# Merged value-output weights of an attention kernel: one block at each layer boundary, or four parts in the layer before

## What is computed

```python
def attn_layer(x, Wqkv, qs, ksc, Wo):
    q, k, v = jnp.split(x @ Wqkv, 3, -1)      # 16 heads of 64
    ...
    out = local_attention(q, k, v)            # softmax(q k) v, windows of 32
    out = out.transpose(0, 2, 1, 3).reshape(b, n, INNER)
    return out @ Wo
for i in range(DEPTH):                        # 6
    x = attn_layer(shift_tokens(x), Wqkv[i], ...) + x
    x = ffn_layer(shift_tokens(x), ...) + x
```

## Time and profile before

| | |
|---|---|
| median of 3 runs | 3483.62 us (3481.26 to 3486.61) |
| the profiled execution | 3489.47 us, its span 3487.7 us |
| mean granted clock of TensorE | 0.986 of full |
| TensorE, VectorE, ScalarE, GpSimd busy | 3341.8, 2797.8, 2306.6, 2258.2 us |
| the recurrence, from the first tanh to the first projection of a layer | 13.8 to 379.8 us |
| the layers | 379.8 to 3487.7 us |

### The profile page before, as it was taken

How to read it: one execution, slowest core, us unless ns; L and a number is a source line. 1 busy time by engine, 2 the same in 40 slices (tenths; PEclk the granted TensorE clock), 3 DMA queues, 4 the chain that set the end, 5 groups by cost and what they waited for, 6 DMA issues and landing times. The chain is left out here.

```text
span 3487.7 us, 101023 instructions
## 1 busy us (share of the span) xinstructions
PE 3341.8 (96%) x42261; PEld 2160.1 (62%) x42261; DVE 2797.8 (80%) x4511; ACT 2306.6 (66%) x4497; POOL 2258.2 (65%) x1364
## 2 busy tenths in 40 slices
PE   8999699999999999999999999999999999999996
PEld 4555366666666666666666666666666666666663
DVE  2333498888898898888898789888898888898983
ACT  2222267777777777777777677776777777777774
POOL 0000267777677777777777677777677776777773
PEclk9999799999999999999999999999999999999999
DMA  2000000100000100001000001000001000000000
GB/s 71 1 1 1 4 11 11 32 11 11 11 13 12 35 11 11 8 17 35 11 11 8 11 17 33 10 11 11 8 17 35 11 11 8 11 17 16 12 11 13
DMA packets 62282, 52.51 MB, mean 15 GB/s; under 512 B 11527, under 2 KB 59397, under 8 KB 61829
## 3 DMA queue, kind: packets, MB, share of 16 engines
q1 hardware_dynamic: 61828, 46.05, 5.1%
HBM read 43.93 MB, written 2.10 MB: 13 GB/s over the span
## 5 line engine op out<-in xcount | busy, mean ns | idle before, releaser
L448 POOL TENSOR_TENSOR cosp<-cosp,rr 128x1024 f32<-128x1024 f32 x384 | 722.6, 1903 | 592.4 <-DVE rr L963 592.3
L458 POOL TENSOR_TENSOR cosp<-cosp,sinp 128x1024 f32<-128x1024 f32 x384 | 902.5, 2370 | 65.9 <-DVE sinp L942 65.9
L543 PE MATMUL ps<-w_qk,xs 128*128 128x512 f32 x1536 | 766.6, 622 | 20.1 <-ACT sq L755 16.5
L644 PEld LDWEIGHTS ps<-px,w_vo 128*128 128x128 f32 x6144 | 701.0, 192 | 57.5 <-ACT px L808 45.7
L644 PE MATMUL ps<-px,w_vo 128*128 128x128 f32 x6144 | 721.4, 276 | 1.9 <-ACT px L808 1.7
L755 ACT ACTIVATE sq<-ps 128x1024 f32<-128x1024 f32 x384 | 392.7, 1023 | 472.9 <-DVE sinp L942 472.9
L939 DVE TENSOR_TENSOR cosp<-ps,tab 128x1024 f32<-128x1024 f32 x384 | 469.3, 1222 | 153.9 <-PE ps L543 152.6
L543 PEld LDWEIGHTS ps<-w_qk,xs 128*128 128x128 f32 x1536 | 264.2, 192 | 387.6 <-issue 378.6
L948 DVE TENSOR_REDUCE ss<-sq 128x16 f32<-128x1024 f32 x384 | 455.3, 1186 | 54.4 <-ACT sq L755 54.3
L942 DVE TENSOR_TENSOR sinp<-ps,tab 128x1024 f32<-128x1024 f32 x384 | 466.4, 1215 | 0.0
L704 PE MATMUL ps<-pT,xtm 32*128 32x512 f32 x3072 | 445.0, 628 | 12.7 <-issue 4.7
(11 more groups left out here) (106 smaller groups left out, 4475.9 us busy)
## 6 DMA issues: line engine op xcount, KB each, us to landing
tab<-in_tab SPq DMA_DIRECT2D x96, 128.0 KB, 2.1
qks<-in_scales SPq DMA_DIRECT2D x96, 128.0 KB, 3.3
w_qk<-in_L_ffn_Wqkv SPq DMA_DIRECT2D x12, 512.0 KB, 6.3
w_v<-in_wv_t SPq DMA_DIRECT2D x6, 512.0 KB, 8.4
w_o<-in_L_ffn_Wo SPq DMA_DIRECT2D x6, 512.0 KB, 9.2
x<-in_L_attn_x SPq DMA_DIRECT2D x16, 128.0 KB, 5.1
out<-w_v SPq DMA_DIRECT2D x16, 128.0 KB, 2.4
w<-in_L_ffn_W SPq DMA_DIRECT2D x6, 341.0 KB
```

The costliest lines, as they stand in the source:

```text
L448: eng.tensor_tensor(v, v, rr[:, B % 2, HEADS * i:HEADS * i + HEADS].unsqueeze(2).to_broadcast([P, HEADS, DH]), ALU.mult).then_inc(rot_read ...
L458: eng.tensor_tensor(cosp[:, A % 2, i, :], cosp[:, A % 2, i, :], sinp[:, i, :], ALU.add).then_inc(rot_added, 1)
L543: t = eng.matmul(ps[:, u, :], xs[:, n % ROUND, :], w_qk[:, n // TILES % 2, i, 512 * u:512 * u + 512], start=True, stop=True)
L644: t = eng.matmul(Y, w_vo[:, i // HP, i % HP, :], px[:, i, :], start=i == 0, stop=i == HEADS - 1)
```

## The change

The block is cut into four parts. For layers 1 to 5 part p of layer L is made in step 32 (L - 1) + 16 + 4 p, so in the first step of each of the last four turns of the layer before. A part has two of the eight 64-row slices, both halves of each: four matmuls into banks G(1) and G(2), 256 columns of each, ahead of that step's Y. One ScalarE copy takes them to `w_vo`, which now has two sets, taken in turn by layers. Layer 0's four parts are made inside the recurrence, at position 24 of chunks 3 to 6, in banks 2 and 6, and VectorE copies them in two instructions each. SyncE asks for the weights of q, k, value and output one turn earlier. To make room, the buffer `xe` of the last turned rows is laid into the output weights' buffer.

```diff
@@ -114,7 +114,7 @@
 LN_STEPS = 3 * TB + 1 + NSTEPS
 POST_STEPS = 1 + LN_STEPS + 3 + LN_STEPS
 KEEP = 512
-AT_OUTPUT, AT_INPUT, AT_XN = 3, 38, 54
+AT_OUTPUT, AT_FUSE, AT_INPUT, AT_XN = 3, 24, 38, 54
 DMA_W1 = 1 + 2 * len(FT)
 DMA_W2 = len(FT) + 1
 
@@ -136,7 +136,7 @@
         w_qk = sb("w_qk", [P, 2, 2, INNER])
         w_v = sb("w_v", [P, HP, D])
         w_o = sb("w_o", [P, HP, D])
-        w_vo = sb("w_vo", [P, 2, HP, D])
+        w_vo = sb("w_vo", [P, 2, 2, HP, D])
         w_1 = sb("w_1", [P, 2 * FF])
         w_2 = sb("w_2", [P, 3, D])
         tab = sb("tab", [P, 2, 4, DH])
@@ -167,7 +167,6 @@
         px = sb("px", [P, HEADS, P])
 
         xc = sb("xc", [P, CH])
-        xe = sb("xe", [P, CH])
         xr = sb("xr", [P, TB, D])
         xn = sb("xn", [P, TB, D])
         xf = sb("xf", [P, CH])
@@ -194,6 +193,7 @@
         t4 = sb("t4", [P, 4, TB])
         b4 = sb("b4", [P, TB], I32)
         fin = w_v.rearrange("p (r j) d -> p r j d", r=2)
+        xe = w_o.rearrange("p k d -> p (k d)")[:, 0:CH]
 
         ps = ctx.enter_context(nc.psum_tensor("ps", [P, 8, 512], F32))
         R = ps[:, 0:2, :]
@@ -293,9 +293,9 @@
             T = (s - lag) // ROUND
             return T if (s - lag) % ROUND == 0 and 0 <= T < TURNS else None
 
-        def layer_of(s):
-            L = (s - 2) // TILES
-            return L if (s - 2) % TILES == 0 and 0 <= L < DEPTH else None
+        def fuse_of(s):
+            L, part = s // TILES + 1, s % TILES // ROUND - 4
+            return (L, part) if s % ROUND == 0 and part >= 0 and L < DEPTH else None
 
         def leaving(s):
             c = (s - 4 * (TURNS - NC) - 15) // ROUND
@@ -402,7 +402,7 @@
                 if L and T % NC == 1:
                     load_1(L)
                     load_2(L)
-                if L + 1 < DEPTH and T % NC == 3:
+                if L + 1 < DEPTH and T % NC == 2:
                     load_qk(L + 1)
                     load_vo(L + 1)
             for c in range(TURNS - FIRST_OUT, NC):
@@ -511,6 +511,18 @@
                 eng.matmul(ps[:, 7, 0:KEEP].rearrange("p (a n) -> p a n", n=P), ident_bf[:, :],
                            ident_bf[:, :].unsqueeze(1).to_broadcast([P, KEEP // P, P]), start=True, stop=True)
 
+            def fuse(L, part):
+                if part == 0:
+                    eng.wait_ge(wv_in, 16 * (L + 1))
+                    eng.wait_ge(wo_in, 16 * (L + 1))
+                if L == 0:
+                    after(eng, vo_evac, part)
+                for i in range(2 * part, 2 * part + 2):
+                    for x in range(2):
+                        rows = slice(64 * x, 64 * x + 64)
+                        t = eng.matmul(ps[:, 5 + x if L else 2 + 4 * x, D * (i % 2):D * (i % 2) + D], w_v[rows, i, :], w_o[rows, i, :], start=True, stop=True)
+                t.then_inc(vo_done, 1)
+
             turn_xn(0)
             eng.wait_ge(abc_out, 1)
             eng.wait_ge(zeroed, 8)
@@ -530,11 +542,14 @@
                     keep_warm()
                     if t == AT_OUTPUT and c:
                         outputs(c - 1)
+                    if t == AT_FUSE and c - 3 in range(4):
+                        fuse(0, c - 3)
                     if t == AT_INPUT and c:
                         turn_input(c - 1)
                     if t == AT_XN and c < NC - 1:
                         turn_xn(c + 1)
             outputs(NC - 1)
+            eng.wait_ge(vo_evac, 4)
 
             def project(n, i):
                 if n % TILES == 0:
@@ -637,27 +652,18 @@
                 if tile(E):
                     eng.wait_ge(px_evac, 3 * (E + 1))
                     eng.wait_ge(px_last, E + 1)
+                    if fuse_of(s):
+                        fuse(*fuse_of(s))
                     if E % TILES == 0:
                         eng.wait_ge(vo_evac, 4 * (E // TILES + 1))
                     after(eng, y_added, E)
                     for i in range(HEADS):
-                        t = eng.matmul(Y, w_vo[:, i // HP, i % HP, :], px[:, i, :], start=i == 0, stop=i == HEADS - 1)
+                        t = eng.matmul(Y, w_vo[:, E // TILES % 2, i // HP, i % HP, :], px[:, i, :], start=i == 0, stop=i == HEADS - 1)
                     t.then_inc(y_done, 1)
-                L = layer_of(s)
-                if L is not None:
-                    eng.wait_ge(wv_in, 16 * (L + 1))
-                    eng.wait_ge(wo_in, 16 * (L + 1))
-                    after(eng, y_added, E + 1)
-                    eng.wait_ge(xt_evac, C + 1)
-                    for i in range(HP):
-                        for x in range(2):
-                            t = eng.matmul(G(2 * x + i // 4)[:, D * (i % 4):D * (i % 4) + D], w_v[64 * x:64 * x + 64, i, :],
-                                           w_o[64 * x:64 * x + 64, i, :], start=True, stop=True)
-                            if i % 4 == 3:
-                                t.then_inc(vo_done, 1)
                 if tile(B):
-                    if L is not None:
-                        eng.wait_ge(vo_evac, 4 * (L + 1))
+                    if fuse_of(s):
+                        L, part = fuse_of(s)
+                        eng.wait_ge(vo_evac, 4 * L + part + 1)
                     eng.wait_ge(rot_ready, 2 * B + 1)
                     turn(B, 0, Q_BANKS)
                 if tile(A):
@@ -828,11 +834,11 @@
                     eng.wait_ge(y_added, ROUND * (T + 1))
                     after(eng, rows_done, T)
                     shifted(xc[:, :].rearrange("p (b t) -> p b t", b=BATCH), xb, slice(0, BATCH), turn_cols(T), turn_cols_before(T), xc_ready)
-                L = layer_of(s)
-                if L is not None:
-                    for k in (0, 2, 1, 3):
-                        eng.wait_ge(vo_done, 4 * L + (2 if k % 2 == 0 else 4))
-                        eng.copy(w_vo[:, k // 2, 4 * (k % 2):4 * (k % 2) + 4, :].rearrange("p i d -> p (i d)"), G(k)).then_inc(vo_evac, 1)
+                if fuse_of(s):
+                    L, part = fuse_of(s)
+                    eng.wait_ge(vo_done, 4 * L + part + 1)
+                    after(eng, y_done, TILES * (L - 1))
+                    eng.copy(w_vo[:, L % 2, :, 2 * part:2 * part + 2, :], ps[:, 5:7, 0:2 * D].rearrange("p x (i d) -> p x i d", d=D)).then_inc(vo_evac, 1)
                 if tile(B):
                     after(eng, sims_done, B)
                     for u, k in enumerate(Q_BANKS):
@@ -869,6 +875,7 @@
 
             def read_result(c):
                 eng.wait_ge(x_updated, DEPTH * NC + c + 1)
+                eng.wait_ge(vo_done, 4 * DEPTH)
                 after(eng, end_turned, c)
                 eng.copy(xe[:, :].rearrange("p (b t) -> p b t", b=BATCH), xa[:, :, 1 + FW * c:1 + FW * c + FW]).then_inc(end_read, 1)
 
@@ -923,6 +930,12 @@
             for c in range(NC - 1):
                 if c:
                     post(c - 1)
+                if c - 3 in range(4):
+                    part = c - 3
+                    eng.wait_ge(vo_done, part + 1)
+                    for x in range(2):
+                        t = eng.tensor_copy(w_vo[:, 0, x, 2 * part:2 * part + 2, :].rearrange("p i d -> p (i d)"), ps[:, 2 + 4 * x, 0:2 * D])
+                    t.then_inc(vo_evac, 1)
                 normalise(c + 1)
             post(NC - 2)
             last = Steps(eng, post_step, (NC - 1) * POST_STEPS)
```

## The result

The change takes 3489.89 us (median of 20 runs, 3483.77 to 3494.02); the kernel before, in as many runs beside it, 3482.07 us (3470.73 to 3488.11). The ratio is 1.002, with a 95% interval of 1.0013 to 1.0028, which is 4.5 to 9.8 us. So the change costs 7.8 us: small, but more than the noise between the two sets of runs.

A forecast was written before the change was run, and what follows sets the result against it. TensorE, busy 96% of the span with almost no gaps, was taken as the bound. 49.0 + 2.5 - 42.3 - 6.5 = +2.7 us against the 3483.62 us median gave 3486.3 us, range 3476 to 3503.

The forecast's parts named there:

- twenty parts: Layers 1 to 5, first step of a turn: each part delays the q transposes 2.45 us, +49.0 us in all.
- recurrence: Layer 0's four parts, chunks 3 to 6: about 0.6 us each in the tanh chain, +2.5 us in all.
- five boundaries: Boundary steps of layers 1 to 5 lose two waits, the burst and following half clock: -42.3 us.
- layer 0's block: Step 2, while the pipeline fills: transposes start earlier without the block, -6.5 us, bounds -7.0 and -5.5.
- The chain: In a part's step, ScalarE copies after square and mask; q transposes wait for it, starting 2.45 us later.
- All of it is in the difference to the clean step: 7.17 to 9.75 us: Boundary steps: everything the change removes was taken as their excess over a 15.53 us step, middle 8.46 us.
- The DMA: Weights asked for one turn earlier: cost nothing, landing in 9.2 us against some 61 us until needed.
- The clock rival: TensorE's twenty stops before the q transposes bring half clock, 1.7 us at nine: +15 us, 3501 us; chance 0.30 (slower).
- the nine stops at L691: Stops of 1.6 to 2.2 us counted in the layers' trace; four said to be followed by slow clock.
- behind Y it is safe: The new stop follows dense Y matmuls, like the first boundary's 2.94 us without slow matmuls; no slow stretch summed.
- Faster through catching up: VectorE and GpSimd use the stops; TensorE recovers 0.6 us or more of each: -9 or more, 3474 us; chance 0.07.
- Faster through an early copy: ScalarE reaches the copy during Y, so a part costs only 0.51 us: -36, 3448 us; chance 0.08.

The follow-up runs named there:

- experiment 1: The change with ScalarE's copy of each part moved ahead of the square of q: 3459.01 us, ratio 0.9932 to the kernel before.
- experiment 2: The change with ScalarE's copy of each part between the square of q and the copy of the transposed x: 3465.99 us, ratio 0.9957 to the kernel before.
- experiment 3: The change with a second ScalarE copy, into a spare tile, ahead of each part's copy in layers 1 to 5: 3511.08 us, ratio 1.0083.
- experiment 4: The change with each part of layers 1 to 5 issuing its four matmuls twice: 3486.62 us, ratio 1.0017 to the kernel before.
- experiment 5: The kernel before, with eleven filler matmuls in each boundary step while TensorE waits for Y's sum: 3470.46 us, ratio 0.9964.
- experiment 7: The kernel of experiment 1, with layer 0's four parts replacing two filler matmuls at their positions in the recurrence: 3453.67 us, ratio 0.9915 to the kernel before.
- experiment 8: The kernel of experiment 7, with layers 1 to 5 made in two parts of eight matmuls instead of four: 3452.52 us, ratio 0.9905 to the kernel before.
- experiment 6: The change with layer 0's weights made in the old block in step 2, no parts in the recurrence: 3492.87 us, ratio 1.0033 to the kernel before.

## Why the prediction was right, and where it was off

**Forecast 3486.3 us, range 3476 to 3503, no change that can be told; measured 3489.9 and a ratio of 1.002.** The terms, forecast and then measured between the two profiled executions:

| term | forecast | measured |
|---|---|---|
| twenty parts | +49.0 | +47.0 (2.42 - 0.07 each) |
| recurrence | +2.5 | +3.0 |
| five boundaries | -42.3 | -41.4 |
| layer 0's block | -6.5 | -7.2 |
| sum | +2.7 | +1.4 |

The spans differ by 0.0. Of the other 1.4 us, 1.0 lie in the second halves of the twenty steps, where the unexplained stops at L691 (L697 after) fall into other steps than before, and 0.4 in the rest of the layers.

**The parts.** The chain was read rightly: transposes 2.45 us late (5.50 to 7.95), as forecast to 0.01, at all twenty. Experiments 1 to 3 move the copy or add to it, and the half step follows; experiment 4 shows that the matmuls do not matter as long as the stop covers them (where it is gone, in experiment 1, they cost 0.76 us). The stop is 1.45 us, not 1.8: the burst pushes the end of Y back by 0.83 us (6.50 us after the step's start, 5.67 before), not by 0.51. That was a wrong size with no effect on the sum, because it is covered.

**The boundaries.** The terms fit the two profiles; what was off is the way from there to the medians, +2.7 forecast against +7.8 measured. The weak step is "All of it is in the difference to the clean step: 7.17 to 9.75 us", and with it that the 5.85 us between profile and median was taken as the same for both kernels. The five differences add up to 42.6 us, and some 12 of them were the half clock of one execution, which another execution need not have. How much of it a median execution of before had cannot be read from one trace. By experiment 5 the medians moved 11.6 us where these steps moved 14.1 in the profiles; an estimate of the boundaries' share in the median is then 28.5 + 11.6 = 40.1 us, 2.2 less than the forecast's 42.3. That is 2 of the 5 us, and the interval of experiment 5 (8 to 17 us) is wide enough for none or for all.

**Layer 0** won 7.2 us in the profile, over the bound of 7.0, and part of that is luck. Its own step gave 6.1, within the bounds. The other 1.1 us are the half step before it, 7.2 us long before and 6.1 after; it is 7.2 again in experiments 7 and 8, where no block stands in step 2 either, so that is not the change's doing. And the 6.1 held half clock like the boundaries: in experiment 6 the same block cost 4.0 us. With these two figures the sum for the medians would be 47.0 + 3.0 - 40.1 - 4.0 = +5.9 us, an estimate that lies inside the measured 4.5 to 9.8. It is not shown: half clock in a median execution was never traced, and experiment 4, with the half steps of the change, lies only 4.7 us over the kernel before. **The recurrence** cost 0.75 us per part and not 0.6, since the burst is 0.71 long there too. **The DMA** never showed.

**The rivals.** The clock rival (3501) did not come in: the matmuls right behind the twenty stops all ran at full clock. It was nearer than I thought. Of the nine stops at L691 five were followed by the slow clock, not four (the fifth is 1.62 us long, with 3.69 us for L704 behind it at 3159.55 us), which at 1.7 us each would have put the rival at 3505, over the top of my range. Stops of 1.93 us, 0.5 longer, had it at six of twenty (experiment 3), so the argument "behind Y it is safe" holds for the size that came and not as a rule. The Trainium skill's rule ("TensorE: Matmul & The Clock Gate", section "Why this matters for your kernels"), by which only a clearly longer stop brings the clock down, does not hold in experiment 3: the trace has half clock behind six of twenty stops of 1.93 us. Faster through catching up: nothing came back in experiment 3, and the 0.07 us per part are there without a stop as well (experiment 1). Faster through an early copy (3448) was what another place of the copy gives: 3459, with 0.25 us more per part than priced.

So the change traded a block of 5.7 us per layer at full clock (28.5 / 5), and some clock, for four stops that cost 9.4 together (four times 2.42 - 0.07). Cutting the work into parts did hide the wait for Y's sum, but each part brought a wait of its own, on an engine that reaches the copy late by program order.

## What to carry to other kernels

When work is moved to where an engine has room, look at where in the order of the helping engine its answer stands. ScalarE had 2.2 us idle in that very step, AHEAD of a square that waits for VectorE; in its place behind the square and the mask the copy cost 31 us more than ahead of them (3489.9 against 3459.0). And a cost that contains half clock should be taken from several executions or measured with the wait filled. Filler matmuls in the old kernel's wait won 11.6 us where this restructuring lost 7.8; with the copy in its better place the restructuring won 23.

## What was not expected of the hardware

A burst of small matmuls has a price of its own: 0.76 us for eight records of 64 rows among others and 1.20 for sixteen, while a burst of 32 on its own is 2.06 us long. Behind the same work, the sixteen matmuls of Y, longer stops were followed by half clock more often: 1.45 us, none of twenty, in each of two profiles (the change and experiment 6); 1.93 us, six of twenty (experiment 3, one profile); 2.6 to 2.9 us, four of five (before, one profile). And where TensorE had two filler matmuls in the recurrence, a burst of nearly their length (0.71 us for 0.59) in their place still cost 0.28 us per position.
